# Attention's own steps due one step earlier in the order of pieces, in a fused attention and recurrence kernel on one core

## The reference, cut to what matters

```
x = x + attention(x, styles)          # 16 heads of 32 channels
x = x + recurrence(x, t_emb)          # gated state space layer, 1024 inner channels, 16 states
# attention, for each sequence and head
xn   = layernorm(x * s1)
q, k = (xn @ Wq.T) * q_dc, (xn @ Wk.T) * k_dc
v    = (xn @ Wv.T) * v_dc * s2
out  = softmax(q @ k.T * scale) @ v
out  = (out @ Ww.T) * w_dc + (v @ Wu.T) * u_dc
```

## Time and profile before

| | |
|---|---|
| three runs | 6448.9, 6457.05, 6458.57 us; median 6457.05 us |
| the profiled execution | 6452.4 us, its span 6450.6 us |
| start of the first `S` of unit 0 | 146.6 us |
| attention's last `C` | 3333.5 us |
| recurrence, after it | 3117 us |
| start of units 9, 10, 11 and 12 | 1050.95, 1155.0, 1247.6 and 1351.0 us |

### The profile page before, as it was taken

How to read it: one execution, slowest core, us unless ns; L and a number is a source line. 1 busy time by engine, 2 the same in 40 slices (tenths; PEclk the granted TensorE clock), 3 DMA queues, 4 the chain that set the end, 5 groups by cost and what they waited for, 6 DMA issues and landing times. The chain is left out here.

```text
span 6450.6 us, 73170 instructions
## 1 busy us (share of the span) xinstructions
PE 6002.0 (93%) x24000; PEld 2740.8 (42%) x24000; DVE 4564.4 (71%) x5830; ACT 2348.0 (36%) x4460; POOL 3206.0 (50%) x2625
## 2 busy tenths in 40 slices
PE   7999999999999999999986869999999999999998
PEld 4444444444444444444434324444444444444343
DVE  4655656555565655555535999998999999998984
ACT  2444444444444444443444323333232323233111
POOL 1776666766657666676655232424334342424313
PEclk7999999999999999999987989999999999999999
DMA  2332313323233231332214234444444344444433
GB/s 87 82 86 74 97 52 96 89 74 94 53 99 89 74 92 45 105 85 64 84 54 132 62 98 107 128 108 113 121 119 126 99 135 99 129 105 114 124 92 113
DMA packets 411564, 613.29 MB, mean 95 GB/s; under 512 B 58768, under 2 KB 189968, under 8 KB 410672
## 3 DMA queue, kind: packets, MB, share of 16 engines
q1 hardware_dynamic: 374320, 558.24, 31.3%
q10 hardware_dynamic: 36864, 50.38, 3.0%
HBM read 305.31 MB, written 201.38 MB: 79 GB/s over the span
## 5 line engine op out<-in xcount | busy, mean ns | idle before, releaser
L1125 POOL TENSOR_TENSOR acc<-acc,prob 128x512 f32<-128x512 f32 x1536 | 1906.6, 1275 | 960.6 <-PE bank L815 728.0
L1055 DVE TENSOR_REDUCE mx<-bank 128x1 f32<-128x512 f32 x2048 | 1314.7, 684 | 588.4 <-PE bank L785 583.7
L2064 DVE SCALAR_TENSOR_TENSOR g<-xps,bd,g 128x1024 f32<-128x1024 f32 x1024 | 1312.7, 1282 | 156.9 <-PE xps L1794 83.8
L948 ACT ACTIVATE prob<-misc 128x512 f32<-128x512 f32 x1496 | 842.7, 597 | 852.4 <-PE misc L802 690.0
L1794 PE MATMUL xps<-sx,spread 128*128 128x512 f32 x2048 | 886.8, 519 | 181.1 <-DVE g L2064 164.4
L785 PE MATMUL bank<-khat,qhat 96*128 96x512 f32 x2048 | 989.7, 534 | 40.0 <-DVE mx L1055 20.5
L2070 DVE TENSOR_SCALAR g<-g,lim 128x1024 f32<-128x1024 f32 x1024 | 881.0, 860 | 32.3
L802 PE MATMUL misc<-qhat,khat 98*128 98x512 f32 x1679 | 724.1, 461 | 58.7 <-ACT prob L948 42.1
L1794 PEld LDWEIGHTS xps<-sx,spread 128*128 128x128 f32 x2048 | 357.0, 195 | 707.5 <-DVE g L2064 387.7
L1808 PE MATMUL yps<-g,cexp 128*32 128x512 f32 x4096 | 603.5, 641 | 0.1
L785 PEld LDWEIGHTS bank<-khat,qhat 96*128 96x128 f32 x2048 | 390.7, 196 | 433.7 <-issue 298.8
(11 more groups left out here) (220 smaller groups left out, 6781.2 us busy)
## 6 DMA issues: line engine op xcount, KB each, us to landing
sx<-scratch_xhl SPq DMA_DIRECT2D x512, 128.0 KB, 4.9
scratch_dx<-dx SPq DMA_DIRECT2D x64, 512.0 KB, 2.7
scratch_xhl<-xhi SPq DMA_DIRECT2D x64, 512.0 KB, 4.2
scratch_xhl<-xn SPq DMA_DIRECT2D x64, 512.0 KB, 4.6
scratch_y<-ysb SPq DMA_DIRECT2D x512, 64.0 KB
dx_t<-scratch_dx SPq DMA_DIRECT2D x59, 512.0 KB, 6.2
y_t<-scratch_y SPq DMA_DIRECT2D x59, 512.0 KB, 3.9
xt_n<-in_x SPq DMA_DIRECT2D x112, 256.0 KB, 3.0
```

Of the source, the lines that this page charges most:

```text
L948: act.activation(to, bank[m][:, 0:QC], ACT.Exp, scale=SCALE).then_inc(sem[f"act_m{m}"], 1)
L1055: dve.tensor_reduce(self.mx2[:, h * TT + qt, c:c + 1], bank[m][:, 0:QC], AX.X, ALU.max).then_inc(sem[f"dve_m{m}"], 1)
L1125: pool.tensor_tensor(self.acc[:, a, h, :], self.acc[:, a, h, :], self.prob[:, (n % 2) * GH + h, :], ALU.add).then_inc(sem["pool_acc"], 1)
L2064: dve.scalar_tensor_tensor(self.g[:, t % 4, :], self.xps[t % 2][:, :], self.bd[:, i % 2, tl:tl + 1], self.g[:, (t - 1) % 4, :], ALU.mult, ...
```

## The change

All pieces that `attend` writes, `S`, `E`, `C`, `A`, `N`, `R`, `I`, `D`, get a `due` that is lower by one step. The side lanes' dues, the gate, the banks and the recurrence's own steps (lower by three already) are as they were. No instruction is added or removed.

```diff
@@ -368,7 +368,7 @@
 
         def put(t, *a, **k):
             put_(*a, **k)
-            out[-1]["due"] = u * n_steps + t
+            out[-1]["due"] = u * n_steps + t - 1.0
         for n in range(n_steps + 3):
             if n < n_steps:
                 c, kt = divmod(n, TT)
```

## The result

The changed kernel takes 6391.2 us, the median of four runs (its profiled execution 6391.6 us, span 6389.8), against 6457.6 us before: a ratio of 0.9898, 95% interval 0.9884 to 0.9911. It is 66 us faster; 35 were forecast. One run of the four met a disturbed clock (9518.5 us) and is left out of the ratio.

What follows compares the result with a forecast made beforehand. PE was taken to set attention's pace, with POOL doing so in g = 2. The terms, -26 + 5 - 21 - 9 - 5 + 22 = -34 us against 6452.4, gave 6418, forecast as a 6422 us median; range 6378 to 6468.

Steps and rivals of the forecast that it cites:

- forecast case: Whole kernel: 15 to 60 us faster, 6397 to 6442 us; chance 0.48.
- term B: Square root, once in each of seven batches: PE's wait shrinks as `E` come ahead; 21 us gained, bounds 0 and 43.
- Term A: `S` waiting for `E` to free its bank: fewer quick reuses; 26 us gained (bounds 13 to 42), 5 us back.
- Term C: POOL in g = 2: one `nb_mul` moves behind the unit's last `A`; 9 us gained, bounds 18 gained, 9 lost.
- Term D: Start of g = 3: all four first `E` ahead of a `cat` on ACT; 5 us gained, bounds 10 gained, 10 lost.
- term E: Side work in lumps: longer runs of `mx` make PE wait for DVE; 22 us lost, bounds 5 and 58.
- Rival 3: PE's clock: the halved wait at the square root leaves it at 2.4 GHz, 23 us more gained, 6398 us; chance 0.13.
- Rival 1: Comes out even: `S` waits less, but the wait moves to `mx` on DVE; 6445 to 6465 us; chance 0.21.
- Rival 2: Slower: DVE takes PE's place as the one waited for; +18 us (6475 us) to +50; chance 0.18.

Runs made afterwards that it cites:

- experiment 1: Kernel before, with the addition ahead of the square root taken off DVE (a `bn_aggr` stands in, the square root adds epsilon as bias): 6417.3 us, 0.9947.
- experiment 3: Kernel before, with the due lower by one step only in units with g = 1: 6416.1 us, 0.9945.
- experiment 4: Kernel before, with the due lower by one step for the score matmuls `S` alone: 6407.3 us, 0.9929.
- experiment 7: Kernel before, with the due of all attention pieces lower by two steps instead of one: 6374.3 us, 0.9884.
- experiment 9: Kernel before, with all attention pieces two steps early in g = 2 and one step early elsewhere: 6337.1 us, 0.9821.
- experiment 10: Kernel before, with pieces two steps early in g = 2, one step in g = 0 and 1, `S` alone one step in g = 3: 6353.5 us, 0.9845.
- experiment 12: Kernel before, with the pieces of units with g = 2 alone two steps early: 6418.8 us, 0.9950.
- experiment 5: Kernel before, with the due lower by one step for all attention pieces but `S`: 6436.5 us, 0.9976.
- experiment 2: Changed kernel, with the addition ahead of the square root taken off DVE in the same way: 6392.9 us, 0.9906 against the kernel before.

## Why the prediction was right, and where its sizes were off

The sign and the kinds of unit held: 66 us came instead of 35, inside the range but outside the forecast case's own 15 to 60, in g = 0 and 1 and hardly in g = 3. Unit 10, which was to stay near 92 us, took 89.8. If the terms add up, 32 of the 60 us in the profiled executions are term B, by experiment 1, where the sum had 21; the other 28 are A, C, D and E together, where the sum had 13 (26 - 5 + 9 + 5 - 22), above all because the loss of term E mostly did not come.

**Term B, the square root, was the mis-sized one.** The step that failed is "Once in each of seven batches DVE spends 3.38 us on the 128x8 addition", and from it "1.2 to 1.4 us of wait, then three more maxima". I took the row's duration for work and kept it in the new order. It was a wait for POOL, and the new order ends it: 5.5 us of unit 9 in place of 3.0. Experiment 1 measured this wait alone at 32 us over the seven units, against 21 forecast, under the upper bound of 43. The earlier trace rows had a hint, a reduction over 128x512 takes 0.68 us; POOL's row, which ends with the addition's, was in the trace and not among the rows. As in the earlier trace rows, nothing shows behind the table load but the load itself: it starts at 1087.23 in the changed kernel and the `E` follows at 1088.53.

The Trainium skill has this rule, and the prediction didn't use it. "SBUF — State Buffer", section "Who interferes with whom", says that VectorE and GpSimd share one pair of ports as an exclusive lock, which a `tensor_scalar` in a 2-port mode takes and a `tensor_reduce` never does. The runs agree so far: the addition was held up beside POOL, while the reductions and the stand-in ran beside it in their usual time in experiment 1 (six reductions in 3.68 us, 0.18 us). That this addition runs in such a mode no run shows. On how long the loser waits the page speaks of the holder's instruction; here the wait was 3.4 us, the rest of one of POOL's additions and two whole ones at 1.25 us each. The measurement decides.

**Rival 3, the clock, came true in its condition.** The low clock in g = 1 went from 41 to 0 us, and its 6398 us (6422 less 23 is 6399) was nearer than 6422. But the wait hadn't been halved, it was gone, and in experiment 1 too both vanished together. So the runs don't split the 32 us between wait and clock; an estimate from the 41 us at half the clock is that it cost some 20 us at most. There are new low stretches too, in g = 2, 65 to 85 us. But experiment 3, in which the pieces of g = 2 keep their old dues, has 85 us there as well, so that lumps of `mx` brought them isn't shown.

**Term A, banks of `S`,** net 21 us: the waits in the earlier trace rows fell by 24. That the two numbers are close is luck in part: the three lines together fell by 64 us, and a wait of PEld is not PE's lost time. The mechanism held only in part. The waits were to fall "by count" and rose from 453 to 485 in that line (545 for 552 in all three), and `S` alone brings g = 0 nothing (experiment 4). Counting uses of a bank on PE leaves out when ACT gets to the `E`.

**Term C, POOL in g = 2,** 9 us gained: 0.4 measured over eight units; unit 10 gained 2.9, and units 14, 18 and 22 lost 1.5 to 3.9 with 17 to 20 us of low clock. End of unit 10 in the changed kernel, POOL and PE, for the earlier trace rows:

```profile
1218.62 4.96 POOL L1125 TENSOR_TENSOR acc<-acc,prob 128x512 f32<-128x512 f32 x4
...
1223.51 1.28 POOL L1108 TENSOR_TENSOR xt_n<-xt_n,brow 128x512 f32<-128x512 f32 x1
1223.63 1.04 PE L831 MATMUL bank<-acc,ones 128*32 128x512 f32 x2 [0.18 <-POOL acc L1125]
```

The `nb_mul` did move behind the last `A`, as the prediction has it. What it left out is when POOL begins. I kept to the end of its queue. In experiments 7, 9, 10 and 12 the first addition comes 6.2 to 8.2 us into the units with g = 2, and these units, the last one left out, take 83 to 88 us; in all other runs it comes at 11.8 us or later, and they take 89 us or more. All pieces of these units were moved together, so that POOL's start is the cause fits the rows but wasn't tested by itself.

**Term E, runs of `mx`,** 22 us lost: in g = 3, where the shown step lies, `mx` comes 1.4 us later per unit (1.5 forecast for the step), 10 us in seven units; in g = 2 it comes 2.0 us later. In g = 0 and 1 it comes earlier. The total of `mx` waits on DVE fell by 9 us instead of rising by 10 to 30; 15 such steps were priced like the one looked at. Rivals 1 and 2 needed that rise and fall with it.

**Term D, start of g = 3,** 5 us. The first `E` all stand ahead of the transfers now, as described. ACT and PE at the start of unit 11 after, for the earlier trace rows:

```profile
1226.03 0.59 ACT L948 ACTIVATE acc<-misc 128x512 f32<-128x512 f32 x1
...
1235.11 4.26 ACTq L547 DMA_DIRECT2D qhat<-halves  x6
...
1241.53 1.04 PE L802 MATMUL misc<-qhat,khat 98*128 98x512 f32 x2
```

`C` of step 0 comes 4.2 us into the unit in place of 17.5, but the `S` at 1241.53, step 2, stands 16.9 us in, and by `C` of step 4 only 1.5 us of the lead are left. In g = 3 the terms D and E can't be told apart: together they gave 0.9 us. The recurrence kept its time to 1.2 us.

## What to carry to other kernels

When a small instruction on VectorE has a long row, compare it with a large one of the same engine and look at what GpSimd does until its end: it may be a wait, which a reorder can remove or bring. Where one engine's queue nearly fills a unit, ask first when it can begin. And gains of single stages don't add up when their seams hand work on: measure the combination.

## What the runs showed that I had not expected

- A 128x8 `tensor_scalar` on VectorE took 3.39 to 3.41 us when it came 0.37 us or so after the start of one of POOL's back-to-back additions (all seven of before, all seven of experiment 12), and 0.16 us with POOL idle. It was passed over at two boundaries between POOL's instructions.
- It was let in at such a boundary when it came just ahead of it: 0.02 us ahead of the next addition's start in experiment 7 (0.17 us, five times), 0.14 us in experiment 5 (0.21 us, six times). The seventh of experiment 5 came 0.29 us ahead and took 2.85 us. What decides wasn't tested by itself.

Experiment 5's group of these:

```profile
L1005 DVE TENSOR_SCALAR rstd<-mv x7: 208/217/2854, 284.7 to 2716.8; 128x8 f32<-128x8 f32 x7
```

- The units with g = 2 differ by up to 8 us among each other in one execution: 89.8, 94.5 and 97.9 us for units 10, 14 and 22 of the changed kernel. Units 10 and 14 have the same order of pieces; unit 22 has another, but took 92.2 us in experiment 2 with its attention order unchanged. In the changed kernel those of 94 us and more had 17 to 20 us of low clock; in experiment 2 unit 10 had 17 us of it and took 92.3 us. Where it starts, and whether it is cause or effect, is open.
